# Sample attention of a four-layer kernel: softmax division and normed rows ahead of the expert choice for three batches

## The reference, cut to what matters

```python
scores = jnp.einsum('sbhd,tbhd->bhst', q, k) * scale
attn = jax.nn.softmax(scores, axis=-1)
ctx = jnp.einsum('bhst,tbhd->sbhd', attn, v).reshape(s_len, bsz, d)
attn_out = ctx @ out_w.T + out_b
x = _ln(src + attn_out, ln1_g, ln1_b)
tok = x.reshape(-1, d)
logits = tok @ gate_w.T + gate_b
probs = jax.nn.softmax(logits, axis=-1)
topv, topi = jax.lax.top_k(probs, K)
topv = topv / jnp.sum(topv, axis=-1, keepdims=True)
```

## Time and profile before

| | |
|---|---|
| median of 3 runs | 1234.88 us (1233.9 to 1239.96) |
| the profiled execution, its own time | 1232.73 us |
| its span in the trace | 1231.0 us |
| the stage "samp" on DVE, from the first `values` to the last counts | 494.8 to 644.0 us of the span |
| DVE / PE / POOL busy over the whole span | 61% / 90% / 42% |
| mean granted clock of TensorE | 0.943 of full speed |

### The profile page before, as it was taken

How to read it: one execution, slowest core, us unless ns; L and a number is a source line. 1 busy time by engine, 2 the same in 40 slices (tenths; PEclk the granted TensorE clock), 3 DMA queues, 4 the chain that set the end, 5 groups by cost and what they waited for, 6 DMA issues and landing times.

```text
span 1231.0 us, 20861 instructions
## 1 busy us (share of the span) xinstructions
PE 1111.4 (90%) x7462; PEld 934.5 (76%) x7462; DVE 751.2 (61%) x1662; ACT 428.1 (35%) x882; POOL 522.0 (42%) x499
## 2 busy tenths in 40 slices
PE   6899799998899998999987999999997899968795
PEld 4688678886688855888987999999995688855564
DVE  2787779997688645888851222222226787636683
ACT  2455432333456511121112222222223356551475
POOL 4544503456477221667766110100364666420342
PEclk9999989999999989899977999999999899987898
DMA  7999400000200020000046332211212100000001
GB/s 275 386 387 387 150 1 1 23 1 1 83 1 1 1 97 0 1 2 26 27 142 237 110 113 95 103 38 38 85 51 57 44 1 1 1 1 0 1 26 43
DMA packets 43732, 93.59 MB, mean 76 GB/s; under 512 B 3821, under 2 KB 17806, under 8 KB 40838
## 3 DMA queue, kind: packets, MB, share of 16 engines
q1 hardware_dynamic: 35254, 62.24, 14.1%
q0 software_dynamic: 7104, 29.14, 6.6%
q10 hardware_dynamic: 1296, 1.18, 0.3%
HBM read 39.02 MB, written 51.51 MB: 74 GB/s over the span
## 4 chain that ended last, share of the span: by engine, by line
PE 69%; DVE 16%; ACT 5%; issue 4%; POOL 4%; DMA 1%; DVEq 0%; SPq 0%; POOLq 0%; ACTq 0%
PE PS L2153 11%; PE PS L2163 10%; PE PS L981 8%; PE PS L2030 4%; PE PS L1675 4%; PE PS L960 4%; PE PS L994 3%; PE PS L950 2%; PE PS L904 2%; PE PS L2019 2%; DVE scr L1174 2%; PE PS L1379 2%; DVE scr L1200 2%; PE PS L2056 1%; PE PS L901 1%
## 5 line engine op out<-in xcount | busy, mean ns | idle before, releaser
L2153 PEld LDWEIGHTS PS<-scr 128*128 128x128 f32 x992 | 118.2, 194 | 5.4 <-issue 1.7
L2153 PE MATMUL PS<-scr 128*128 128x128 f32 x992 | 120.3, 279 | 1.6 <-ACT scr L2181 1.3
L2186 ACT ACTIVATE scr<-PS,W 128x128 f32<-128x128 f32 x148 | 53.5, 367 | 192.6 <-PE PS L2153 192.6
L643 POOL TENSOR_TENSOR scr<-scr,small 128x1232 f32<-128x1232 f32 x32 | 71.8, 2245 | 102.3 <-DVE small L443 102.3
L2163 PE MATMUL PS<-scr 128*128 128x256 f32 x496 | 112.2, 379 | 0.0
L768 ACT ACTIVATE big<-PS 128x512 f32<-128x512 f32 x144 | 74.1, 524 | 85.8 <-PE PS L960 85.1
L2216 DVE TENSOR_SCALAR scr<-PS,W 128x128 f32<-128x128 f32 x148 | 51.3, 350 | 84.3 <-PE PS L2153 84.3
L2163 PEld LDWEIGHTS PS<-scr 128*128 128x128 f32 x496 | 91.8, 190 | 11.2
L2222 DVE TENSOR_TENSOR scr<-PS,W 128x256 f32<-128x256 f32 x37 | 15.7, 425 | 125.8 <-PE PS L2163 121.9
L960 PE MATMUL PS<-W,scr 128*128 128x128 f32 x480 | 78.8, 282 | 14.2 <-ACT scr L763 4.1
L981 PEld LDWEIGHTS PS<-scr,big 128*128 128x128 f32 x640 | 81.2, 191 | 6.8 <-issue 4.9
(11 more groups left out here) (410 smaller groups left out, 2488.2 us busy)
## 6 DMA issues: line engine op xcount, KB each, us to landing
expert_in<-zeros SPq DMA_DIRECT2D x1, 19712.0 KB, 55.7
expert_out<-zeros SPq DMA_DIRECT2D x1, 19712.0 KB, 106.9
scr<-ew_in POOLq DMA_DIRECT2D x12, 1024.0 KB, 6.4
scr<-expert_in SPq DMA_DIRECT2D x38, 128.0 KB, 2.0
big<-ew_in POOLq DMA_DIRECT2D x4, 1024.0 KB, 8.3
expert_out<-scr POOLq DMA_DIRECT2D x28, 128.0 KB, 2.0
W<-pack SPq DMA_DIRECT2D x1, 2458.0 KB, 8.6
W<-pack SPq DMA_DIRECT2D x1, 2152.0 KB, 9.4
```

The costliest lines, as they stand in the source:

```text
L643: g.tensor_tensor(sc3, sc3, a_mx[u % 3].unsqueeze(2).broadcast_to([P, H, S2]), ALU.subtract).then_inc(s["sub_ready"], 1)
L2153: ins = pe.matmul(bank(1 + f % 4, G), e_w1[slot][:, k, f * P:(f + 1) * P], e_xT[:, k, :], start=(k == 0), stop=(k == C - 1))
L2186: a.activation(e_h[:, f, :], bank(1 + f % 4, G), ACT.Relu, bias=moe_bias(e, f)).then_inc(s["h_act"], 1)
```

## The change

Three things are moved, all for the first three batches (`LATE = 3`). In the iteration of the choice, DVE now runs the division and the normed rows first and `picked` last. `shared` (and ACT's exponential for it) comes at the end of the iteration after. Ranks on PE and `slots` on DVE come one iteration later than before: iterations 8, 12 and 16. The last two batches keep their places, and so does the table `SCATTERED`.

```diff
+        LATE = 3
+
+        def picked_last(it, lag):
+
+            q = batch_at(it, lag)
+            return q if q is not None and q < LATE else None
+
+        def ranked_at(it):
+
+            early, late = batch_at(it, 4), picked_last(it, 5)
+            return late if early is None or early < LATE else early
+
...
-                q_slot, q_pick = batch_at(it, 4), batch_at(it, 3)
+                q_slot, q_pick = ranked_at(it), batch_at(it, 3)
+                q_late, q_share = picked_last(it, 3), picked_last(it, 4)
                 if q_slot is not None:
                     slots(q_slot, it > UNITS)
                 if q_pick is not None:
                     logits_read(q_pick, it > UNITS)
                 if 1 <= it <= UNITS:
                     measured(it - 1)
-                if q_pick is not None:
+                if q_pick is not None and q_late is None:
                     picked(q_pick)
                 if it + 1 < UNITS:
                     probs(it + 1)
                 if it < 2:
                     v.sem_inc(s["row8_ready"], 1)
-                if q_pick is not None:
+                if q_pick is not None and q_late is None:
                     shared(q_pick)
                 if 2 <= it < UNITS:
                     normed(it - 2)
+                if q_late is not None:
+                    picked(q_late)
+                if q_share is not None:
+                    shared(q_share)
...
                 q = batch_at(it, 3)
+                if q is None or q < LATE:
+                    q = picked_last(it, 4)
                 if q is not None:
                     n = BATCHES[q][1] - BATCHES[q][0]
                     a.wait_ge(s["top_ready"], q + 1)
...
-                u, x, q = it - 1, it - 3, batch_at(it, 4)
+                u, x, q = it - 1, it - 3, ranked_at(it)
```

## The result

| | before | changed |
|---|---|---|
| median | 1234.99 us (4 runs, 1233.9 to 1239.96) | 1254.73 us (4 runs, 1248.04 to 1257.45) |
| the profiled execution, its own time | 1232.73 us | 1254.62 us |
| its span | 1231.0 us | 1252.9 us |
| mean granted clock of TensorE | 0.943 | 0.929 |

The change makes the kernel slower: ratio 1.0148, 95% interval 1.0116 to 1.018, some 18 us. The forecast was 1238.8 us, with a range up to 1243.0.

The account below looks back on a forecast made before the run. It aimed at DVE's 2.75 us wait for PE's sum, with POOL's scatters bounding the stage's end. Holds and lateness summed to +3.9 us, 2.5 from queued scatters: 1234.88 + 3.9 = 1238.8 us, range 1232.0 to 1243.0.

Parts of the forecast that it names:

- the mechanism: DVE instructions with both inputs in SBUF stand until POOL's running product ends: L1837 held 3.8 us, L1858 near 4.4.
- the first batch: Iterations 6 to 8: values(7) 3.0 us late, values(8) 6.9, values(9) 3.7, after two holds and a removed wait.
- B: No long holds, small operands slip in: DVE gains 6, queued scatters cost 3; -2.9, 1232.0 us; chance 0.14.
- C: First batch: the share's L1846 slips in before product(10) reads; values(9) 1.7 late, end +2.2, 1237.1 us; chance 0.10.
- The step that failed: Second batch: the choice ends at 587.05, product(13) starts at 587.6, so the choice runs in a gap.
- rival A: Second batch: product(13) holds the last running counts; values(11) 5.2 later, +3.5 more, +7.4 in all, 1242.3 us; chance 0.16.
- The shift between the holds: Lateness of values: 3.7 us at values(9), falling to 3.1 in the second batch.
- The wait removed has paid for half of the two holds: Iteration 8: DVE's 2.75 us wait for PE's sum disappears, so values(9) is only 3.7 late after values(8)'s 6.9.
- The tail: Stage end: unit 8's two scatters queue ahead of unit 15's deviation, 3.9 us late; 2.5 of it the scatters.
- 1.5 either way: Allowance in us around the forecast for noise from PE's clock, as half clock over 3 us costs half of it.

Follow-up runs that it names:

- e12: The kernel before, unchanged, timed and traced again: 1234.55 us (10 runs), ratio 0.9998.
- e2: Changed kernel with POOL's products of iterations 7 and 11 also waiting for the choice: 1243.37 us (10 runs), ratio 1.0015.
- e4: Changed kernel with units 2 and 3 both scattered in iteration 10, none in 11: 1248.24 us (10 runs), ratio 1.0045.
- e9: Changed kernel with only POOL's product of iteration 11 (unit 13) waiting for the choice: 1249.43 us (4 runs), ratio 1.0121.
- e10: Changed kernel with only POOL's product of iteration 7 (unit 9) waiting for the choice: 1250.96 us (4 runs), ratio 1.0132.
- e7: Changed kernel with LATE = 2, so the third batch keeps its old places: 1250.94 us (6 runs), ratio 1.0071.
- e5: The changed kernel, unaltered, timed again: 1249.78 us (10 runs), ratio 1.0077.
- e8: Kernel before with 14 chained small POOL operations ahead of the last scatters, a delay of 8.8 us: 1246.85 us, ratio 1.0036.
- e1: Changed kernel with the share put ahead of the normed rows again, still one iteration late: 1251.87 us (4 runs), ratio 1.0091.
- e3: Changed kernel with share ahead of the normed rows and POOL's products of iterations 7 and 11 behind the choice: 1241.51 us (10 runs), ratio 1.0001.
- e6: Changed kernel with share first, POOL's products of iterations 7 and 11 behind the choice, and LATE = 2: 1240.62 us (10 runs), ratio 1.0005.

## Why the prediction was wrong

**Right: the mechanism, and the first batch.** `values(7)`, `(8)` and `(9)` were to be 3.0, 6.9 and 3.7 late, and were 2.9, 6.9 and 3.6. L1837 took 3.75 (foretold "near 3.9"), L1858 4.30 ("near 4.4"), both are plain in the third batch, PE's sum was no longer waited for, and L1790 of the second batch, which met a product's end, took 1.26, a hold of 0.97 (0.9 foretold). That `values(9)` fits to 0.1 is in part luck: against e12 it is 5.2 late (see below). Rivals B and C fall: e2, e4, e9 and e10 switch the holds on and off with the product's position, and a small instruction doesn't slip in. The rule of the Trainium skill (SBUF — State Buffer, "Who interferes with whom"), that of a VectorE instruction with two SBUF inputs and a GpSimd instruction that reads SBUF the second to issue waits until the first finishes, gives here the full rest of a product; the trace agrees for L1837 and L1858, with 3.75 and 4.30 us for 8 columns. The count with 5.24 us is shown to start before the product, and yet it is the one that was held, so by the shown starts alone the rule would have let it pass.

**The step that failed.** "product(13) starts at 587.6. The choice ends at 587.05." From this the forecast concluded that no instruction of the second batch's choice would be held. Both stamps were nearly right in distance: in the changed kernel the counts would have ended at about 588.75 and the product is shown from 589.27, a margin of 0.5 where I had 0.55. But the margin was not enough: the fourth count took 5.24 us, held from before the product's shown start on, and that cost the stage 4.1 us. My own rival A had the place, and its condition in the wrong terms ("if DVE is 0.6 later"), which is why it got 0.16. Its `values(11)`, 5.2 later than forecast (8.3 in all), is what came: 89.0 to 97.5. The rows of before left a gap that I didn't weigh: no hold in the earlier trace rows says when a product begins to hold, only when it ends.

**The terms that were mis-sized.** Rival A's sum was +7.4, the stage lost 12.1. By the runs:

- *The held count*: 4.1 (e9), where A had 3.5 (its own terms, 5.2 less 1.5, give 3.7). Right enough.
- *The shift between the holds*, that is, how late `values` is without the held count. I let it fall to 3.1 in the second batch, without a sum for it. In e9, which has no held count, it is 3.6 at `values(9)`, 3.4 at `values(11)`, and 5.7 at `values(13)`: PE waits for `values(11)` and its sum then takes 6.73 us at half clock where it had 4.55. At `values(15)` it is 4.8, not 2.2: 2.6 short. The cause, as far as these profiles tell, is that I took one execution's spells of half clock for fixed. Against e12 the shift is nearly flat: 5.2 at `values(9)`, 5.0 at `(11)`, 5.8 at `(13)`, 4.9 at `(15)`. "The wait removed has paid for half of the two holds" was bought with the 1.6 us by which that wait was longer in the execution I read (2.75, e12: 1.13).
- *The tail*: 1.7 between `values(15)` and the end by the forecast (3.9 less 2.2). e9 has 2.8 (7.6 less 4.8). e7 shows that the third batch's delay is worth 3.5 in the stage, where I had 2.5 for its scatters.

Together 3.9 + 2.6 + 1.1 + 4.1 = 11.7, the stage's loss in e5 against before (171.9 less 160.2); the profiled changed kernel has 0.4 more, which I didn't follow up.

**Outside the stage** the forecast had nothing, and "1.5 either way" for the clock. In the profiled pair it was 9.8 us (1.6 ahead, 8.2 behind), and 6.0 of that lie in the stretch up to the next attention, where L904 runs at half clock. e5 against e12 has 11.7 in the stage, 0.6 in that stretch, 1.3 after it, and 0.3 less ahead of the stage. So the first difference of 19.7 us holds the 12 that the change costs in the stage and some 8 that the profiled pair puts down mostly to the clock and that it does not cost every time: e5's median is only 8.6 over before. The kernel before varies in the same manner, with medians of 1234.6 to 1241.2 in the different sets of runs. e9 and e10 have shorter stages than e5 and yet medians 13.9 and 15.4 over the kernel before, since that stood at 1235.56 in their set and at 1241.15 in e5's; so the whole times can't rank versions from different sets. The stage's 12 us are shown; how much of them an average execution feels is open. The two measurements of the changed kernel give ratios of 1.0077 and 1.0148.

**What stays open.** Which execution gets the slow start of the next attention, and what makes e8's two clusters. And from which moment exactly a queued product holds DVE: at least 0.5 us before its shown start, and no more than some 0.7 before it in the changed kernel, where the third count passed. A smaller operand in the place of the held count, or one that is read from PSUM, wasn't tried.

## What to carry to other kernels

Before an instruction of DVE with both inputs in SBUF is moved, lay it over POOL's long SBUF instructions: if it begins inside one, or would end up to some 0.5 us before the shown start of one that is queued without a wait, count the rest of that instruction as its price, whatever its own size, and then ask whether another wait hides it (e1). In this kernel an order that releases POOL's work earlier did no harm once POOL waited for such instructions: that was worth 9 us in the stage (e2), 12 with the share moved too (e3), and the reordering itself 2 (e6). And read the kernel before in two executions: DVE's wait for PE's sum behind a spell of half clock differed by 1.6 us between them, and a forecast that spends such a wait can be off by that much.

## What the runs showed of the hardware that I had not expected

- A DVE `tensor_tensor` on 128x8 that would have ended 0.5 us *before* POOL's product is shown to start took 5.24 us, to the product's end. With a semaphore wait ahead of the product (e9) and the same distance in the profile (1.29 and 1.28 us from the first count to the product) it took its plain time.
- POOL's scatters, right beside such instructions, hold nothing (e4: four counts in 0.77 us beside a scatter). Nor do its operations on one column: in the kernel before L1833, a `tensor_tensor` with both inputs in SBUF, took its plain 0.19 us at 580.81, inside POOL's L192 (580.64 to 581.21).
- TensorE's waits of 5.46 and 7.78 us behind a hold were followed by half clock for 6.8 and 10.3 us, where the kernel before had 6.8 and 3.4. In the second batch the stall of DVE was so paid for a second time on PE.
- The same kernel, on the same chip, has runs 6 us apart (e8: 1241 to 1242 and 1246 to 1253). The profiles fall in two groups by whether a spell of half clock lies in L838, where a wait for DVE hides it, or at L904, where it makes the stretch up to the fixed product some 5 us longer (301.2 to 303.5 against 307.1 to 308.5).
